# A two-layer graph network on one core: GpSimd's low-half subtraction in the build waits for VectorE's one-hots

## The chip, the core and the metric

The kernel runs on one core of a Trainium2 chip. The metric is the device time of one execution in microseconds (us). The core has five engines: TensorE (PE in the profile), VectorE (DVE), ScalarE (ACT), GpSimd (POOL) and SyncE (SP), which here issues the DMAs. Each runs its own list of instructions in order, and they wait for each other on semaphores.

## The reference

A graph of 3125 nodes with 256 features and 50,000 edges goes through two layers:

```python
def _layer(x, rows, cols, vals, W, b):              # vals = 1 / degree of the row
    neigh = segment_sum(vals[:, None] * x[cols], rows)
    cat = concatenate([x, neigh], axis=1)
    return relu(cat @ W.T + b)

h = _layer(_layer(x, src, dst, vals, W0, b0), src, dst, vals, W1, b1)
x = layernorm(x + h)
h_sparse = keep_32_largest(x @ W_neigh)
neigh = segment_sum(h_sparse[src], dst) / maximum(degree(dst), 1)
x = layernorm(x + x @ W_self + neigh)
```

## The kernel before

The nodes are 25 tiles of 125 (`NT`, `P`). All sums over neighbours are matrix products with the dense matrix of edge counts, `ct`, 3125 x 3125 in float16, that the kernel makes itself in its first part, the build (about 20 to 171 us). The layers then multiply `ct` with the features, which are kept as two float16 parts, high and low, side by side in `xs` (512 columns a tile).

The build has one round per tile (`fills` for TensorE, the branch under `total > E - 1` for VectorE, `quick_copies` for ScalarE, `split_a0` for GpSimd). In the round of tile t:

- VectorE makes four sets of one-hots for tile t + 1 (`quick_hots`, L663, a comparison of `iota128` with `jobs`, both in SBUF): a large one (125x1792) and three smaller ones (125x1536). Between them it copies two groups of transposed counts out of PSUM into `ct` (`tr_copy`, L820). The order is large one-hots, copy, three sets of one-hots, copy. Every set increments `win_hot`. In rounds 4 and 5 it also computes two low parts of weights (`w_low`, L815).
- TensorE multiplies the one-hots of tile t into counts (`fill`, L1388), transposes the counts of the tile before (`transposes`, L1468), computes the rows' own product with the first weights in float32 (`own_product`, L1502) and transposes the next tile of x (L1483).
- ScalarE copies the counts from PSUM to `slab` (L1095), half of the transposes to `ct` (L1134), the own product to `own` (`own_copy`, L1152) and the transposed x to `x_t` (L1139).
- GpSimd splits the second half of `own`, the scaled x, into its two parts in `xs`: a cast makes the high part (L542), a subtraction the low part (L544). The cast waits for ScalarE's copy (`own_copied`), the subtraction for the cast (`a0_hi`). The subtraction increments `a0_split`.
- SyncE stores `own` and `slab` to DRAM.

The split has `own` with two halves, so ScalarE's copy of tile t waits for the subtraction of tile t - 2:

```python
act.wait_ge(a0_split, t + 1)     # the count starts at 2
```

After the build TensorE starts the first layer's aggregation when `a0_split` shows 23 tiles done, and finishes it when all 25 are.

If the inputs don't fit the quick way (`total < E`), another branch builds the matrix; with these inputs it isn't entered.

Of the kernel before, what the change touches and what calls it, by code (L numbers as in the profile page):

```python
# [30 lines left out]
NT = N // P  # L31
# [14 lines left out]
FILLS = len(SETS)  # L46
# [35 lines left out]
def gnn(nc, x, src, dst, w0, b0, w1, b1, wself, wneigh, out):  # L82
    ctx = ExitStack()
    with ctx:
        sem_names = set()

        def sem(name):
            assert name not in sem_names
            sem_names.add(name)
            return ctx.enter_context(nc.semaphore(name))  # L90
# [186 lines left out]
        win_hot, win_done, win_read = sem("win_hot"), sem("win_done"), sem("win_read")  # L277
# [202 lines left out]
        def _(pool):  # L480
# [52 lines left out]
            def split_a0(t):  # L533

                pool.wait_ge(own_copied, t + 2)
                if t == 0:
                    pool.wait_ge(scale_ready, 1)
                    nc.gpsimd.tensor_tensor(own[:, 0, :], own[:, 0, :], scales[0:P, 1:2].broadcast_to([P, 2 * F]), ALU.mult
                                            ).then_inc(own_scaled, 1)
                    pool.wait_ge(own_scaled, 1)  # L540
                a0 = own[:, t % 2, F:2 * F]
                nc.gpsimd.tensor_copy(xs[:, t, 0:F], a0).then_inc(a0_hi, 1)  # L542
                pool.wait_ge(a0_hi, t + 1)
                nc.gpsimd.tensor_tensor(xs[:, t, F:2 * F], a0, xs[:, t, 0:F], ALU.subtract).then_inc(a0_split, 1)  # L544

            pool.sem_inc(a0_split, 2)
            for t in range(NT):
                split_a0(t)
# [43 lines left out]
        def _(dve):  # L592
# [10 lines left out]
            def whole_part(out, given, size, step):  # L603
                step(v.tensor_scalar(out, given, 1.0 / size, 0.5 / size - 0.5, ALU.mult, ALU.add))
                step(v.tensor_scalar(out, out, ROUND, -ROUND, ALU.add, ALU.add))
# [109 lines left out]
            def general_table():  # L715

                count = [0]

                def step(ins):
                    count[0] += 1  # L720
                    ins.then_inc(slow_step, 1)
                    dve.wait_ge(slow_step, count[0])

                dve.wait_ge(win_hot, 2 * FILLS)
                dve.wait_ge(win_done, FILLS)
                by_chunk = [edges_f[:, j, 0:EQ * P].rearrange("p (g q) -> p g q", g=EQ) for j in range(2)]
                whole_part(hi_f[:, 1], by_chunk[1], W, step)
                whole_part(hi_f[:, 0], by_chunk[0], P, step)
                step(v.scalar_tensor_tensor(key[:, :, :], hi_f[:, 1], float(NT * W - W), by_chunk[1], ALU.mult, ALU.add))
                step(v.scalar_tensor_tensor(srcp[:, :, :], hi_f[:, 0], -float(P), by_chunk[0], ALU.mult, ALU.add))  # L730
                step(v.scalar_tensor_tensor(key[:, :, :], hi_f[:, 0], float(W), key[:, :, :], ALU.mult, ALU.add))
                v.engine_nop().then_inc(edge_keys, 2)
                step(v.tensor_reduce(wlim[:, 1, :], hi_f[:, 1], X, ALU.max))
                step(v.tensor_reduce(wlim[:, 0, :], hi_f[:, 1], X, ALU.min))
                for j in range(2):
                    for g in range(EQ):
                        last = v.tensor_scalar(wdiag[:, j, g, :], identf[0:EG, 0:EG], wlim[:, j, g:g + 1], None, ALU.mult)
                last.then_inc(diag_ready, 1)
                dve.wait_ge(keys_t, 1)
                step(v.memset(key_t[:, CH:CH + G], -1.0))  # L740
                step(v.memset(srcp_t[:, CH:CH + G], 0.0))
                for out, b in ((srcp_t, bank[0]), (key_t, bank[1])):
                    step(v.tensor_copy(out[:, 0:CH].rearrange("p (e g) -> p g e", g=EQ),
                                       b[0:P, 0:CH].rearrange("p (g e) -> p g e", g=EQ)))

                dve.wait_ge(lims_b, 1)
                step(v.tensor_scalar(cover[:, :], bank[2][0:P, 0:CH], wcol[:, :], None, ALU.is_le))
                step(v.scalar_tensor_tensor(cover2[:, :], bank[3][0:P, 0:CH], wcol[:, :], cover[:, :], ALU.is_ge, ALU.mult))
                step(v.tensor_tensor(cover3[:, :], cover2[:, :], rev_f[:, :], ALU.mult))
                step(v.tensor_tensor(cover4[:, :], cover2[:, :], inc_f[:, :], ALU.mult))  # L750
                step(v.tensor_reduce(lim[:, 0:1], cover3[:, :], X, ALU.max))
                step(v.tensor_reduce(lim[:, 1:2], cover4[:, :], X, ALU.max))
                step(v.tensor_scalar(lim[:, 2:3], lim[:, 0:1], -1.0, float(CH), ALU.mult, ALU.add))
                step(v.tensor_tensor(lim[:, 3:4], lim[:, 1:2], lim[:, 2:3], ALU.subtract))
                step(v.tensor_scalar(lim[:, 4:5], lim[:, 3:4], 1.0 / G, (G - 1.0) / G + 0.5 / G - 0.5, ALU.mult, ALU.add))
                step(v.tensor_scalar(lim[:, 5:6], lim[:, 4:5], ROUND, -ROUND, ALU.add, ALU.add))
                v.tensor_scalar(lim[:, 6:7], lim[:, 5:6], 1.0, None, ALU.max).then_inc(win_lims, 1)

                dve.wait_ge(rows_t, 1)
                step(v.memset(rows[:, :, :], 0.0))  # L760
                step(v.memset(rows[:, 3, :], 1.0))
                step(v.tensor_copy(rows[:, 0, 0:NW], bank[4][0:1, 0:NW]))
                step(v.tensor_copy(rows[:, 2, 0:NW], bank[4][0:1, 128:128 + NW]))
                step(v.tensor_tensor_scan(rows[:, 1, 1:NW + 1], rows[:, 3, 0:NW], rows[:, 2, 0:NW], 0.0, ALU.mult, ALU.add))
                v.tensor_copy(table[:, :, :], rows[:, 0:2, :]).then_inc(table_ready, 1)
# [129 lines left out]
            with dve.If(total < E):  # L895
                general_table()
                clear_tr()
                bound_rows()
                bounds()
                scales_out()  # L900
                for u in range(WT):
                    general_hots(u)
                for i in range(4):
                    w_low(i)
                with dve.Fori(1, NT) as t:
                    for u in range(WT):
                        general_hots(t * WT + u)
                        if u == 1:
                            v.tensor_copy(xstage[:, :], xs32[:, ds(t - 1, 1), :].rearrange("p o f -> p (o f)")).then_inc(own_staged, 1)
                first_trees()  # L910
# [69 lines left out]
            for T in range(NT):  # L980
                b, K = T % 2, T - 3
                t = t2[(NT + T) % 2]
# [740 lines left out]
```

## Time and profile before

| | us |
|---|---|
| median of three runs | 665.47 |
| lowest, highest | 664.07, 667.5 |
| the profiled execution's own time | 663.18 |
| its span, first to last instruction | 661.4 |

| engine | busy us | share of the span |
|---|---|---|
| TensorE, matmuls | 629.1 | 95% |
| VectorE | 496.6 | 75% |
| ScalarE | 314.2 | 48% |
| GpSimd | 111.6 | 17% |

The shares are averages over parts with different limits. In the page's 40 slices VectorE and ScalarE are at nine tenths or more from the fifth slice to the tenth, within the build, and TensorE is so in nearly all slices. In a row in order of time the first number is the start in us from the span's start and the second how long the instruction, or the merged group of them, took. Records of instructions that follow each other closely on one engine overlap by some hundredths of a microsecond. What an engine waited for stands in brackets.

### The profile page before, as it was taken

The page shows a single profiled execution, that of the slowest core. Times are in us where ns is not written, and L with a number is a line of the kernel's source. Part 1 is how long each engine was busy: PE and PEld are TensorE (multiplying, and loading weights), DVE is VectorE, ACT ScalarE, POOL GpSimd, SP SyncE. Part 2 cuts the span into 40 slices and gives each one's busy share as a digit, 9 for nine tenths or more (in the row PEclk, how much of TensorE's full clock was granted, in tenths as well). Part 3 has the DMA queues.
Part 4 walks back from the last instruction along what each step waited for, and adds up shares of the span by engine and source line. Part 5 has one row for each costly group of instructions (what it writes and reads, how often), then busy time and mean ns, then how long its engine had stood idle before and what let it go on. Part 6 is the DMA issues. An engine that isn't in the chain of part 4 may idle for free.

```text
span 661.4 us, 10805 instructions
## 1 busy us (share of the span) xinstructions
PE 629.1 (95%) x3758; PEld 321.4 (49%) x3759; DVE 496.6 (75%) x1273; ACT 314.2 (48%) x606; POOL 111.6 (17%) x188
## 2 busy tenths in 40 slices
PE   7789999999888999999999999998999999999996
PEld 3466677666433444444444444444444444444442
DVE  7988999999688888888853687886888837533333
ACT  3779999999486676757641222222222200000000
POOL 3014222112211010101101223223232200000000
PEclk9989999999999999999999999999999999999999
DMA  9435655555422232322213999999999633300000
GB/s 230 90 116 154 223 182 173 169 179 181 134 50 64 51 67 49 67 51 64 55 45 110 204 180 186 196 175 204 181 196 189 152 97 115 111 25 27 24 24 24
DMA packets 66742, 79.62 MB, mean 120 GB/s; under 512 B 30320, under 2 KB 59407, under 8 KB 66681
## 3 DMA queue, kind: packets, MB, share of 16 engines
q1 hardware_dynamic: 66681, 78.86, 53.6%
q8 instruction: 32, 0.52, 0.4%
q14 instruction: 29, 0.24, 0.1%
HBM read 38.91 MB, written 33.38 MB: 109 GB/s over the span
## 4 chain that ended last, share of the span: by engine, by line
PE 54%; DVE 32%; DMA 6%; ACT 3%; issue 2%; POOL 2%; SPq 0%; ACTq 0%; DVEq 0%; POOLq 0%
PE pair L1575 22%; DVE hots L663 12%; PE bank L1673 11%; PE pair L1673 10%; DMA tr_sb<-part 5%; DVE ct L820 4%; PE pair L1476 3%; PE bank L1476 3%; DVE m L966 3%; DVE work L971 2%; PE bank L1502 1%; DVE tree L849 1%; DMA own_in<-own_dram 1%; POOL part L571 1%; PE bank L1468 1%
## 5 line engine op out<-in xcount | busy, mean ns | idle before, releaser
L1575 PE MATMUL pair<-xs,ct 125*128 125x512 f16 x625 | 139.5, 379 | 1.2 <-issue 1.2
L1575 PE MATMUL pair<-a,ct 125*128 125x512 f16 x625 | 138.9, 379 | 0.0
L663 DVE TENSOR_TENSOR hots<-iota,jobs 125x1792 f16<-125x1792 f16 (+1 forms) x100 | 103.1, 1066 | 0.8 <-ACT jobs L1077 0.7
L1575 PEld LDWEIGHTS pair<-a,ct 125*128 125x128 f16 x625 | 62.0, 99 | 73.8
L1575 PEld LDWEIGHTS pair<-xs,ct 125*128 125x128 f16 x625 | 61.7, 100 | 73.9 <-issue 1.7
L1254 ACT ACTIVATE a<-ct 125x1000 f16<-125x1000 f16 (+1 forms) x75 | 80.4, 1071 | 9.6 <-DMA c_dram<-slab 7.9
L1095 ACT ACTIVATE slab<-pair 125x875 f16<-125x875 f32 (+1 forms) x100 | 83.3, 860 | 3.1 <-PE pair L1388 1.6
L553 POOL TENSOR_TENSOR own_in<-own_in,bias_sb 125x256 f32<-125x256 f32 x50 | 38.5, 771 | 235.9 <-DMA own_in<-own_dram 235.8
L1673 PE MATMUL bank<-xs,ct 125*128 125x512 f16 (+1 forms) x325 | 71.5, 379 | 0.0
L1673 PE MATMUL pair<-xs,ct 125*128 125x512 f16 x300 | 66.2, 379 | 0.0
L1322 ACT ACTIVATE sd<-mv,epsb 125x1 f32<-125x1 f32 x25 | 7.4, 294 | 113.9 <-DVE mv L1028 113.9
L1468 PEld LDWEIGHTS bank<-ident,slab 125*128 125x128 f16 x625 | 39.6, 99 | 35.9 <-issue 22.1
L925 DVE SCALAR_TENSOR_TENSOR t<-pair,rdeg,own_in 125x256 f32<-125x256 f32 x50 | 24.1, 483 | 43.4 <-PE pair L1575 38.2
L1388 PE MATMUL pair<-hots 125*128 125x125 f16 x625 | 52.5, 223 | 3.9 <-DVE hots L663 3.1
L1468 PE MATMUL bank<-ident,slab 125*128 125x125 f16 x625 | 51.5, 220 | 4.8 <-ACT slab L1095 1.7
L1502 PE MATMUL bank<-w_t,x_t 128*125 128x512 f32 x100 | 53.6, 621 | 1.5 <-DVE sv L782 0.9
L1673 PEld LDWEIGHTS bank<-xs,ct 125*128 125x128 f16 (+1 forms) x325 | 32.3, 100 | 37.8
L1673 PEld LDWEIGHTS pair<-xs,ct 125*128 125x128 f16 x300 | 29.8, 99 | 34.9
L1388 PEld LDWEIGHTS pair<-hots 125*128 125x128 f16 x625 | 40.6, 100 | 7.7 <-issue 4.7
L1476 PE MATMUL bank<-w_lay,tr_sb 128*128 128x512 f16 x150 | 36.5, 379 | 4.6 <-DMA tr_sb<-part 4.5
L1476 PE MATMUL pair<-w_lay,tr_sb 128*128 128x512 f16 x150 | 36.5, 379 | 3.2 <-DMA tr_sb<-part 3.1
L820 DVE COPY ct<-bank 125x1008 f16<-125x1008 f16 x50 | 33.6, 671 | 7.6 <-PE bank L1468 7.6
(203 smaller groups left out, 750.2 us busy)
## 6 DMA issues: line engine op xcount, KB each, us to landing
c_dram<-slab SPq DMA_DIRECT2D x25, 683.6 KB
ct<-c_dram SPq DMA_DIRECT2D x25, 683.6 KB
own_in<-own_dram SPq DMA_DIRECT2D x50, 125.0 KB
own_dram<-own SPq DMA_DIRECT2D x25, 125.0 KB
own_dram<-own_st SPq DMA_DIRECT2D x25, 125.0 KB
x_in<-in_x_dram SPq DMA_DIRECT2D x25, 125.0 KB
z_dram<-z_st SPq DMA_DIRECT2D x25, 125.0 KB
a<-z_dram SPq DMA_DIRECT2D x5, 625.0 KB
```

Source lines behind the costliest of these rows:

```text
L553: nc.gpsimd.tensor_tensor(own_in[k % 2][:, :], own_in[k % 2][:, :], bias_sb[:, :], ALU.add).then_inc(own_biased, 1)
L663: v.tensor_tensor(hots[k][:, :, :, :].rearrange("p w g (a d) -> p (w g) a d", d=2), iota, job, ALU.is_equal).then_inc(win_hot, 1)
L820: v.tensor_copy(ct[:, TG0[g]:TG0[g] + TG[g], t, :], tr16[1][0:P, 0:TG[g], 0:PC]).then_inc(tr_free[1], 1)
L925: return noted(v.scalar_tensor_tensor(t2[k % 2][:, :], agg[k % 3][0:P, 0:F], rdeg[l][:, T:T + 1], own_in[k % 2][:, :], ALU.mult, ALU.add))
L1095: a.activation(slab3[t % 2][:, :, lo * QW:hi * QW].rearrange("p b (w d) -> p b w d", d=QW), pair[f % 2][0:P, 0:n, 0:QKEY].rearrange("p w ( ...
L1254: a.activation(unread[:, 0:(hi - lo) * P].rearrange("p (b s) -> p b s", s=P), ct[:, lo:hi, T, 0:P], ACT.Copy, accum_out=deg_part[:, T, k:k ...
L1388: last = mm(pair[f % 2][:, u, 0:QKEY], hots[f][:, u, 0, :], hots[f][:, u, 1, 1:QKEY + 1], start=True, stop=True, skip_group_check=True)
L1468: last = nc.tensor.transpose(tr16[g % 2][:, i, 0:P], slab[par][:, (TG0[g] + i) * P:(TG0[g] + i) * P + 128], ident16[:, 0:P])
L1476: last = mm(out, lhs(2 * pt + h), w[:, h, q, :], start=h == 0 and k == 0, stop=h == 1 and k == 2, skip_group_check=True)
L1502: last = mm(bank[6][0:P, :].rearrange("p (a f) -> p a f", a=2), x_t32[:, h, :], w0_t[:, h::2, :], start=h == 0, stop=h == 1, skip_group_ch ...
L1575: ins = mm(agg[k % 3][0:lhs.shape[1], :], lhs, parts[l][:, t, :], start=t == 0, stop=t == NT - 1, skip_group_check=True)
L1673: ins = mm(out3[T % 8][0:lhs.shape[1], :], lhs, xs[:, b, :], start=b == 0, stop=b == NT - 1, skip_group_check=True)
```

## The change

GpSimd's subtraction for tiles 4 to 23 waits, beside the cast before it, until `win_hot` has reached 4 (t + 2), that is, until VectorE has finished the fourth set of one-hots for tile t + 1. The branch that isn't entered raises the semaphore by itself, so that GpSimd doesn't wait there for ever. The order of the instructions on every engine stays.

```diff
@@ split_a0(t), GpSimd
                 nc.gpsimd.tensor_copy(xs[:, t, 0:F], a0).then_inc(a0_hi, 1)
                 pool.wait_ge(a0_hi, t + 1)
+                if 3 < t < NT - 1:
+                    pool.wait_ge(win_hot, FILLS * (t + 2))
                 nc.gpsimd.tensor_tensor(xs[:, t, F:2 * F], a0, xs[:, t, 0:F], ALU.subtract).then_inc(a0_split, 1)
@@ general_table(), VectorE
                 dve.wait_ge(win_hot, 2 * FILLS)
+                dve.sem_inc(win_hot, FILLS * NT)
                 dve.wait_ge(win_done, FILLS)
```

## Rows read from the trace of the kernel before

**Rows 1.** Busy time by window, 72.6 to 160.6 us: stretch, length, busy time by engine

```profile
72.60:160.60 88.00, 85.81 (x942) 60.59 (x940) 88.00 (x102) 84.36 (x135) 18.87 (x35) 1.00 0.58 181
```

**Rows 2.** Chain of waits over a tile: start, length, what

```profile
99.04 2.97 DVE hots L663 x3
102.01 0.59 DVE ct L820
102.61 1.00 DVE hots L663
```

**Rows 3.** Order of time, VectorE and GpSimd, the tile at 66 us

```profile
66.64 1.31 DVE L663 TENSOR_TENSOR hots<-iota,jobs 125x1536 f16<-125x1536 f16 x1
...
68.53 1.81 DVE L663 TENSOR_TENSOR hots<-iota,jobs 125x1536 f16<-125x1536 f16 x2
...
66.46 0.67 POOL L544 TENSOR_TENSOR xs<-own,xs 125x256 f16<-125x256 f32 x1
```

**Rows 4.** Order of time, VectorE and GpSimd, two steady tiles

```profile
98.37 0.67 DVE L820 COPY ct<-bank 125x1008 f16<-125x1008 f16 x1
98.96 3.05 DVE L663 TENSOR_TENSOR hots<-iota,jobs 125x1536 f16<-125x1536 f16 x3
...
104.12 3.08 DVE L663 TENSOR_TENSOR hots<-iota,jobs 125x1536 f16<-125x1536 f16 x3
...
98.31 0.40 POOL L542 CAST xs<-own 125x256 f16<-125x256 f32 x1 [4.00 <-ACT own L1152]
98.79 0.67 POOL L544 TENSOR_TENSOR xs<-own,xs 125x256 f16<-125x256 f32 x1
...
103.98 0.67 POOL L544 TENSOR_TENSOR xs<-own,xs 125x256 f16<-125x256 f32 x1
```

**Rows 5.** Order of time, VectorE and GpSimd, the tiles at 60 and 156 us

```profile
60.97 1.16 DVE L815 SCALAR_TENSOR_TENSOR w_parts<-w_t,scales,w_parts 128x512 f16<-128x512 f32 x1
...
64.38 0.74 DVE L815 SCALAR_TENSOR_TENSOR w_parts<-w_t,scales,w_parts 128x512 f16<-128x512 f32 x1
...
155.86 3.24 DVE L663 TENSOR_TENSOR hots<-iota,jobs 125x1536 f16<-125x1536 f16 x3
...
60.30 1.29 POOL L544 TENSOR_TENSOR xs<-own,xs 125x256 f16<-125x256 f32 x1
...
156.16 1.26 POOL L544 TENSOR_TENSOR xs<-own,xs 125x256 f16<-125x256 f32 x1
```

**Rows 6.** All instructions of line L820: shortest, median, longest in ns

```profile
L820 DVE COPY ct<-bank x50: 662/670/684, 37.2 to 170.5; 125x1008 f16<-125x1008 f16 x50
```

**Rows 7.** Order of time, VectorE, the large one-hots of rounds 6 and 23

```profile
71.52 1.08 DVE L663 TENSOR_TENSOR hots<-iota,jobs 125x1792 f16<-125x1792 f16 x1
...
159.62 1.07 DVE L663 TENSOR_TENSOR hots<-iota,jobs 125x1792 f16<-125x1792 f16 x1
```

**Rows 8.** Order of time, where GpSimd answers VectorE

```profile
46.05 0.15 DVE L801 COPY scales<-bank 128x16 f32<-128x16 f32 x1
...
46.36 1.04 POOL L538 TENSOR_TENSOR own<-own,scales 125x512 f32<-125x512 f32 x1 [27.33 <-DVE scales L801]
...
170.46 0.68 DVE L820 COPY ct<-bank 125x1008 f16<-125x1008 f16 x1 [0.78 <-PE bank L1468]
...
171.26 1.10 POOL L559 MEMSET part<- 32x512 f16 x2 [4.36 <-DVE ct L820]
```

**Rows 9.** Order of time, ScalarE and TensorE in one tile

```profile
102.72 0.72 ACT L1152 ACTIVATE own<-bank,scales 125x512 f32<-125x512 f32 x1
103.61 0.38 ACT L1139 ACTIVATE x_t<-bank 128x250 f32<-128x250 f32 x1 [0.17 <-PE bank L1483]
...
102.75 0.60 PE L1468 MATMUL bank<-ident,slab 125*128 125x125 f16 x8
```

**Rows 10.** Chain of waits at the end of the build

```profile
159.84 0.60 PE bank L1468 x8
...
165.00 0.60 PE bank L1468 x8
```

## The prediction

> **What bounds the kernel now.** I first looked at the page's busy shares in slices, to see which engines are full in the build, the part that the change touches. Then I read the busy times by window over that part [rows 1]: in 88.0 us VectorE is busy for all 88.00, ScalarE for 84.36, and TensorE for 85.81, which is a modelled number. The chain of waits over one tile says the same in another way [rows 2]: the only owners are VectorE's three one-hot instructions (2.97 us together), the copy out of PSUM (0.59), the one large one-hot (1.00), and the second copy. So in the build a microsecond that VectorE loses is a microsecond of the kernel, as long as no other engine becomes the bound.
>
> Next I put VectorE's and GpSimd's instructions in order of time beside each other. In the tile at 66 us [rows 3] GpSimd's subtraction runs from 66.46 to 67.13 in its usual 0.67. The one-hots that start at 66.64 inside it take 1.31 us, while the next two, with GpSimd silent, take 1.81 for both. Records overlap by about 0.07, so one clean instruction takes 0.94 and three clean ones take 1.81 + 0.87 = 2.68. VectorE lost 1.31 - 0.94 = 0.37. The steady tiles show the same [rows 4]: three one-hots take 3.05 beside a subtraction that began 0.17 before them, and 3.08 beside one that began 0.14 before them. That is a loss of 0.37 to 0.40, and in other tiles 0.36 to 0.41; I take 0.385. The loss is what was left of the subtraction when the one-hots began, less about 0.06. Two other tiles show the reverse order [rows 5]. There the subtraction starts inside a one-hot instruction, is itself stretched (1.29 and 1.26 for 0.67), gets in when that instruction ends, and delays VectorE's following one: by 1.16 - 0.74 = 0.42 in the tile at 60 us and by 3.24 - 2.68 = 0.56 in the tile at 156 us.
>
> The copy out of PSUM doesn't mind. All 50 lie between 662 and 684 ns [rows 6], though GpSimd's 0.40 us cast and the first part of its subtraction run beside one of them in every tile, themselves at their usual time [rows 4].
>
> **The change, part by part.** It adds one wait, on the count of one-hots, to 20 subtractions (tiles 4 to 23). The subtraction of tile t now starts when the fourth set of one-hots of tile t + 1 is done. In VectorE's order the copy of the other transposes follows there, then the large one-hot of the next tile, so the subtraction leaves the three one-hots and lies beside a copy.
>
> What it removes: in tiles 4 and 5, 0.42 and 0.37. For tiles 6 to 22 I take the distance from one large one-hot to the same one 17 tiles later [rows 7]: 159.62 - 71.52 = 88.10 us, or 5.18 a tile. Sixteen of these lose 0.385 and one loses 0.56: 6.72 us. In tile 23 VectorE's one-hots are no longer on the chain of waits, so nothing is counted there.
>
> What it adds: the subtraction starts some time after the fourth one-hots. GpSimd has answered VectorE twice near the build [rows 8]: a small copy ended at 46.20 and GpSimd started at 46.36, and a copy ended at 171.14 and GpSimd started at 171.26. So the start is 0.12 to 0.16 after, and the end 0.79 to 0.83 after. The copy's share of the chain is 0.59, and then the large one-hot wants to start. By the 0.06 found above its delay is 0.14 to 0.18; I take 0.15. No row shows a subtraction in this place, so the bounds are 0 (the copy covers it whole) and 0.25 (an answer 0.1 slower).
>
> VectorE's time for the 17 tiles becomes 88.10 - 6.72 + 17 x 0.15 = 83.93, or 4.94 a tile.
>
> What is late next: ScalarE idles (88.00 - 84.36) / 17 = 0.21 a tile [rows 1], so from there it needs 4.97; its records overlap by about 0.1 where nothing is waited for, so the true need is a little less, near 4.92. Its one wait is before its copy of the transposed x [rows 9]: TensorE's eight transposes start 0.15 after VectorE's copy (102.60 to 102.75), the transposes of x come behind them, and ScalarE starts at 103.61, 0.17 after it had finished. That wait moves forward with VectorE, so it shrinks. VectorE's 4.94 and ScalarE's 4.92 are almost equal, and I take 4.95 for the tile: 17 x 4.95 = 84.15, a gain of 3.95. Tiles 4 and 5 give 0.42 + 0.37 - 2 x 0.15 = 0.49. There VectorE also splits weights and has no idle time, so it all counts. The last tile runs by TensorE and ScalarE from one group of eight transposes to the next, 165.00 - 159.84 = 5.16 [rows 10]; at 4.95 it gives 0.2. Together 3.95 + 0.49 + 0.2 = 4.6 us.
>
> Behind the waiting subtraction GpSimd has the cast of the next tile, which comes about 3 us after the new start of the subtraction. ScalarE's copy of tile t + 2 waits for the subtraction of tile t; it is given up a whole tile ahead of its need, since `own` has two halves. The wait itself costs GpSimd nothing that matters, because it idles most of each tile. The 25th tile keeps its old order, so the layer's start isn't held up. The added increment in the general branch isn't executed. Everything after the build hangs on its end through the chain of waits, so I pass the gain through whole.
>
> The profiled execution took 663.18 us (span 661.38 and 1.8 around it), so its successor would take 658.6. It lies 2.3 under the median of the three runs, 665.47; against that median the forecast is 660.9. With the added delay at 0 the one-hots' loop is faster than ScalarE, the tile takes 4.92, and the gain is 4.46 + 0.79 + 0.24 = 5.5. With 0.25 a tile takes 5.04, and the gain is 2.5 + 0.3 + 0.1 = 2.9.
>
> **The rivals.**
>
> *The other engines keep the pace.* If the fixed answers between VectorE, TensorE and ScalarE leave half of ScalarE's wait in place, a tile takes about 5.10: 17 x 0.08 + 0.49 + 0.05 = 1.9 gained, 663.6. For it speaks that three loops lie within 0.05 us of each other; against it, that the wait before ScalarE follows VectorE's copy directly.
>
> *The cast takes the place.* The cast (0.40) sits in the shelter of the copy today [rows 4]. If ScalarE's copy of the own product comes 0.5 later against VectorE's order, the cast falls on the first one-hots and costs 0.40 - 0.06 = 0.34. A tile would take 4.94 + 0.34 = 5.28, 0.1 more than now: +1.7 for the 17 tiles less 0.2, so 667.0. Against it: the drift would have to be larger than ScalarE's whole idle time.
>
> *The subtraction comes in front of the large one-hot.* This is the slower side. If the subtraction runs only once the copy has ended, the large one-hot waits for all of it: 0.67 - 0.06 = 0.61 a tile. 17 x 0.61 - 6.72 = +3.65, and in tiles 4 and 5 2 x 0.61 - 0.79 = +0.43: 669.6. It decides from the point where the subtraction starts over 0.38 us after the fourth one-hots (0.38 + 0.67 - 0.06 - 0.59 = 0.40, today's loss); the two answers in the trace are 0.12 and 0.16. The other way to it would be a copy that holds GpSimd off; the rows beside it say no [rows 4, 6]. The Trainium skill (SBUF — State Buffer, Who interferes with whom) lists `copy` among the operations that can take the port pair shared with GpSimd, and says that the loser of it blocks fully. Taken alone that would give this rival's 669.6; the same page ties it to operand conditions, and this copy reads PSUM. The trace stands against it: cast and subtraction keep 0.40 and 0.67 beside the copy.
>
> *There is nothing to remove.* If the stretched one-hots had another cause than the subtraction, their loss would stay and the time would be 665.5. [...] The trace disagrees: 0.94 alone and 1.31 beside a subtraction, and 1.29 for a subtraction of 0.67 [rows 3, 5].
>
> **How the numbers follow.** A measurement of this kernel can tell about 0.5%, 3.3 us, from no change. The forecast has 0.73, the pace of the other engines 0.11, the cast 0.05, the subtraction in front of the large one-hot 0.06, nothing to remove 0.05. Of the forecast's 0.73 I put 0.06 within 0.5%, since its low end gains 2.9. Faster: 0.67. Within 0.5%: 0.06 + 0.11 + 0.05 + 0.05 = 0.27. Slower: 0.06. The range starts at the largest gain, 5.5 under the median, less the 1.4 by which the fastest of the three runs lies under it, rounded in by 0.3: 658.3. It ends at 665.2, where the forecast's low end (662.6) with the 2.0 of the slowest run over the median, and the rival of the other engines' pace (663.6) with most of it, are inside.
>
> **What the profile would show.** Right: three one-hots at 2.68 in tiles 6 to 22, subtractions of 0.67 beginning about 0.15 after the fourth one-hots, beside a copy of 0.67, the large one-hot at about 1.2 for 1.07, a tile of 4.95, and ScalarE's wait before the copy of the transposed x nearly gone. Wrong: a subtraction stretched to over 1 us or a large one-hot near 1.7 (the slower side); one-hots at 3.05 with no subtraction beside them (nothing to remove); one-hots stretched beside the cast; VectorE idle before its copies with tiles over 5.05 (another engine's pace); or a gain in the build that is lost between its end and that of the kernel.

## The result, and the profile after

| | before | after |
|---|---|---|
| median, us | 665.18 (10 runs) | 661.09 (10 runs) |
| lowest, highest | 663.06, 669.77 | 659.55, 662.98 |
| the profiled execution's span | 661.4 | 658.1 |

The ratio of the times is 0.9938, with a 95% interval of 0.9916 to 0.9961: 4.1 us faster. The forecast was 4.6 us faster, at 660.9. The medians here and below leave out four slow executions, one each of e3_write_only, e5_short_own, e6_gate_from_3 and the kernel before, run beside the last two.

First VectorE and GpSimd in order of time, in two steady tiles of the changed kernel. They answer to [rows 4].

```profile
97.48 2.68 DVE L665 TENSOR_TENSOR hots<-iota,jobs 125x1536 f16<-125x1536 f16 x3
100.08 0.67 DVE L823 COPY ct<-bank 125x1008 f16<-125x1008 f16 x1
100.67 1.25 DVE L665 TENSOR_TENSOR hots<-iota,jobs 125x1792 f16<-125x1792 f16 x1
101.85 0.67 DVE L823 COPY ct<-bank 125x1008 f16<-125x1008 f16 x1
102.44 2.68 DVE L665 TENSOR_TENSOR hots<-iota,jobs 125x1536 f16<-125x1536 f16 x3
...
100.31 0.67 POOL L546 TENSOR_TENSOR xs<-own,xs 125x256 f16<-125x256 f32 x1 [2.73 <-DVE hots L665]
102.12 0.40 POOL L542 CAST xs<-own 125x256 f16<-125x256 f32 x1 [1.14 <-ACT own L1155]
```

Three one-hots take 2.68, as when nothing is beside them. The subtraction begins at 100.31, 0.15 after the fourth one-hots ended at 100.16. It runs beside the copy and reaches 0.3 into the large one-hot, which takes 1.25 for 1.07.

The window that answers to [rows 1] (stretch, length, then busy time of TensorE, its weight loads, VectorE, ScalarE and GpSimd):

```profile
72.60:155.60 83.00, 82.53 (x928) 60.62 (x929) 82.94 (x101) 82.32 (x134) 18.29 (x33) 1.00 0.60 188
```

ScalarE idles 0.68 in 83 us, where it idled 3.64 in 88. All three engines are full now. In the chain of waits over a tile, the counterpart of [rows 2], VectorE is gone and TensorE holds every piece, one right behind the other (start, length, what):

```profile
100.37 0.91 PE bank L1505 x2
101.28 0.44 PE bank L1471 x8
```

That doesn't make TensorE the bound. Where three engines are all full, the chain stays on the one on which it is entered; over 98 to 109 us of e1_third the same view names ScalarE alone. The pace is told by the starts. TensorE in order of time:

```profile
98.74 1.08 PE L1505 MATMUL bank<-w_t,x_t 128*125 128x512 f32 x2
...
103.67 1.07 PE L1505 MATMUL bank<-w_t,x_t 128*125 128x512 f32 x2
```

TensorE's round takes 4.93 here, while VectorE's large one-hots (100.67 and, not shown, 105.63) stand 4.96 apart. TensorE is making up a delay that is told below; from about 136 us on its rounds take 4.95 to 4.96 too. So it is still VectorE that sets the steady tile: 4.79 with nothing stretched, and 0.17 for the large one-hot.

The large one-hots of rounds 6 and 23, in order of time, answer to [rows 7]:

```profile
70.75 1.08 DVE L665 TENSOR_TENSOR hots<-iota,jobs 125x1792 f16<-125x1792 f16 x1
...
155.22 1.25 DVE L665 TENSOR_TENSOR hots<-iota,jobs 125x1792 f16<-125x1792 f16 x1
```

They stand 84.47 us apart, where they stood 88.10 apart: 3.63 us in 17 tiles. The first took 4.78, since its large one-hot (70.75) isn't stretched, and two were disturbed. The first of the two in order of time:

```profile
84.72 0.92 ACT L1098 ACTIVATE slab<-pair 125x875 f16<-125x875 f32 x1 [0.68 <-DMA c_dram<-slab]
...
87.21 2.88 DVE L665 TENSOR_TENSOR hots<-iota,jobs 125x1536 f16<-125x1536 f16 x3
...
87.44 0.97 POOL L542 CAST xs<-own 125x256 f16<-125x256 f32 x1 [1.69 <-ACT own L1155]
```

ScalarE waited 0.68 for the store of an earlier slab, so its copy of the own product came late, and the cast behind it fell on the one-hots: 2.88 for 2.68. That is the rival of the cast, once in 20 tiles. This tile took 5.16. The next took 5.11, because TensorE was late and VectorE's copy behind the large one-hot waited for its transposes (0.14). Together the two lost 0.35.

### The profile page after: what moved, and what is told of

Its sections match the earlier page's. It is cut to its first block, busy times and chain, and to the rows that moved or that the text cites. A ratio compares the mean times of both kernels' runs of the same rounds, so it can differ in the third digit from the quotient of the medians.

```text
span 658.1 us, 10825 instructions
## 1 busy us (share of the span) xinstructions
PE 627.2 (95%) x3758; PEld 322.1 (49%) x3759; DVE 492.5 (75%) x1273; ACT 313.2 (48%) x606; POOL 111.5 (17%) x188
## 4 chain that ended last, share of the span: by engine, by line
PE 64%; DVE 16%; DMA 8%; ACT 6%; issue 3%; POOL 2%; SPq 1%; ACTq 0%; DVEq 0%; POOLq 0%
PE pair L1578 22%; PE bank L1676 11%; PE pair L1676 10%; PE bank L1505 5%; DMA tr_sb<-part 5%; PE bank L1471 4%; PE pair L1391 4%; PE bank L1479 3%; PE pair L1479 3%; DVE m L969 3%; DVE work L974 2%; ACT slab L1098 2%; DMA own_in<-own_dram 1%; POOL part L573 1%; DVE tree L852 1%
## 5 line engine op out<-in xcount | busy, mean ns | idle before, releaser
L665 DVE TENSOR_TENSOR hots<-iota,jobs 125x1792 f16<-125x1792 f16 (+1 forms) x100 | 99.1, 1027 | 0.7 <-ACT jobs L1080 0.7
L852 DVE TENSOR_TENSOR tree<-tree,ct 125x630 uint16<-125x630 uint16 x75 | 38.4, 511 | 2.6
```

Source lines behind the costliest of these rows:

```text
L665: v.tensor_tensor(hots[k][:, :, :, :].rearrange("p w g (a d) -> p (w g) a d", d=2), iota, job, ALU.is_equal).then_inc(win_hot, 1)
L852: step(v.tensor_tensor(tree[:, :], tree[:, :], quint[k], ALU.add))
```

## The experiments

Eleven kernels ran. In the profile of each I read one number that hardly depends on what happens elsewhere: the distance over 17 tiles, from the large one-hot of round 6 to that of round 23. The ratios and intervals are those on record; they are not the quotients of the medians beside them.

| kernel | 17 tiles, us | a steady tile | median, us | ratio to before, interval |
|---|---|---|---|---|
| before | 88.10 | 5.16 to 5.19 | 665.2 | |
| the change | 84.47 | 4.96 | 661.09 | 0.9938 [0.9916, 0.9961] |
| e7_change_again | 84.11 | 4.96 | 661.46 | 0.9956 [0.9933, 0.9979] |
| e1_third | 83.84 | 4.92 | 661.12 | 0.9946 [0.9920, 0.9972] |
| e6_gate_from_3 | 83.54 | 4.93 | 661.79 | 0.9950 [0.9927, 0.9973] |
| e3_write_only | 83.73 | 4.93 | 659.79 (4 runs) | 0.9934 [0.9903, 0.9964] |
| e5_short_own | 83.74 | 4.93 | 659.83 (3 runs) | 0.9906 [0.9874, 0.9939] |
| e10_short_product | 82.06 | 4.82 | 659.44 | 0.9916 [0.9884, 0.9947] |
| e11_both_short | 82.57 | 4.79, up to 132 us | 656.85 (4 runs) | 0.9892 [0.9845, 0.9938] |
| e2_second | 88.56 | 5.26 | 665.96 | 1.0027 [1.0002, 1.0052] |
| e4_late | 88.05 | 5.20 | 664.55 | 0.9992 [0.9971, 1.0014] |
| e8_later | 86.53 | 4.99 and 5.29 in turn | 663.45 | 0.9983 [0.9964, 1.0002] |
| e9_cast_gated | 87.52 | 5.16 | 664.60 | 0.9993 [0.9972, 1.0014] |

The median of the kernel before, run beside them, was 665.22, 665.21 and 664.94 in the three groups. In e3_write_only, e5_short_own, e10_short_product and e11_both_short a part of the work is left out, so their times are no measure of the change.

### Is the conflict one of reads?

```diff
-                nc.gpsimd.tensor_tensor(xs[:, t, F:2 * F], a0, xs[:, t, 0:F], ALU.subtract).then_inc(a0_split, 1)
+                if 3 < t < NT - 1:
+                    nc.gpsimd.memset(idle[:, :], 0.0)
+                    nc.gpsimd.memset(xs[:, t, F:2 * F], 0.0).then_inc(a0_split, 1)
```

This edit is made to the kernel before (its other tiles keep the subtraction), without the gate.

> The kernel before, without the gate; in tiles 4 to 23 two memsets (320 and 256 float16 a partition) stand in the place of the subtraction, so the low half is zero there. GpSimd is busy as long as with the subtraction, over the start of the first of the three one-hots, but only writes. Theory (the conflict is over reads: one-hots have two inputs in SBUF, the subtraction too): no one-hots are stretched, three take 2.68 and the large one 1.07; the tile is ScalarE's and TensorE's 4.93, the kernel 4.5 to 5.5 us faster than before. Rival (any GpSimd work on SBUF stretches VectorE): three one-hots at 3.0 and the time of the kernel before.

VectorE and GpSimd in order of time, in e3_write_only:

```profile
106.67 2.69 DVE L668 TENSOR_TENSOR hots<-iota,jobs 125x1536 f16<-125x1536 f16 x3
...
106.42 0.40 POOL L543 CAST xs<-own 125x256 f16<-125x256 f32 x1 [3.86 <-ACT own L1157]
106.87 0.36 POOL L546 MEMSET idle<- 125x320 f16 x1
107.17 0.31 POOL L547 MEMSET xs<- 125x256 f16 x1
```

GpSimd writes from 106.87 to 107.48, inside the first of the one-hots, where a subtraction is held and then delays the next. Neither is stretched: the memsets take 0.36 and 0.31, the one-hots 2.69, as alone. So GpSimd's being busy doesn't stretch VectorE; the subtraction, which reads two inputs from SBUF, does. The Trainium skill (SBUF — State Buffer, Who interferes with whom) states that a VectorE instruction with two SBUF inputs contends with a GpSimd instruction that reads SBUF, and not with one that only writes. The trace agrees: 2.69 for three one-hots beside memsets here, and 1.31 for 0.94 for one beside a subtraction in [rows 3]. A memset differs from a subtraction in more than its reads, so this run alone doesn't prove that it is them; e9_cast_gated below adds that a cast, which reads one input, is held as well. The kernel was 5.4 us faster than before by the medians and 4.4 by the ratio; expected were 4.5 to 5.5.

### What the place costs: the gate earlier and later

The gate one set earlier (e1_third; in e2_second the last line has - 2, two sets earlier):

```diff
-                    pool.wait_ge(win_hot, FILLS * (t + 2))
+                    pool.wait_ge(win_hot, FILLS * (t + 2) - 1)
```

> The gate opens one set earlier, at the third of the four sets of one-hots. Theory (the one who comes second waits for the running instruction, then goes first): the subtraction arrives about 0.15 us after the fourth set has begun, is held to about 1.5 us in its record, gets in as the fourth set ends and runs beside the copy, about 0.1 us earlier than with the gate at the fourth. The three smaller one-hots stay at 2.68, the large one falls from 1.25 to 1.10 or less. VectorE then needs about 4.8 a tile, ScalarE and TensorE 4.93, so the tile takes 4.93 to 4.95 for 4.97 and the kernel 0.3 to 0.7 us less than the change. Rival (VectorE alone bounds the tile): 4.80 a tile, 2.9 us less than the change. Rival (a held subtraction stretches VectorE's instruction): three one-hots at 3.05, time as before the change.

In order of time, in e1_third:

```profile
104.06 0.68 DVE L823 COPY ct<-bank 125x1008 f16<-125x1008 f16 x1
104.66 2.69 DVE L665 TENSOR_TENSOR hots<-iota,jobs 125x1536 f16<-125x1536 f16 x3
107.28 0.67 DVE L823 COPY ct<-bank 125x1008 f16<-125x1008 f16 x1
107.87 1.07 DVE L665 TENSOR_TENSOR hots<-iota,jobs 125x1792 f16<-125x1792 f16 x1
109.00 0.68 DVE L823 COPY ct<-bank 125x1008 f16<-125x1008 f16 x1
...
106.63 1.25 POOL L546 TENSOR_TENSOR xs<-own,xs 125x256 f16<-125x256 f32 x1 [1.83 <-DVE hots L665]
```

The subtraction arrives at 106.63 inside the fourth one-hots, is held, and ends at 107.88, just as the large one-hot begins at 107.87. Nothing of VectorE's is stretched: 2.69 and 1.07. The distance from the large one-hot to the copy behind it is now 1.13, not 1.00, because the copy waits for TensorE, whose eight transposes begin at 108.35 and take 0.60. The tile is 4.92 and not VectorE's 4.80, so the first rival falls. In whole times it can't be told from the change (661.12 and 661.09).

> The gate opens two sets earlier, at the second of the four sets. Theory: the subtraction arrives while the third set runs, is held, and runs just before the fourth, which loses 0.56 as at 156 us in the kernel before. Three one-hots take about 3.24, the large one 1.07, a tile 5.35: 0.17 x 17 = 2.9 us more than the kernel before for tiles 6 to 22, about 668. Rival (only the share of time that the two overlap counts, whatever the order): the loss is at most today's 0.385 and the time that of the kernel before.

In order of time, in e2_second:

```profile
103.49 3.15 DVE L665 TENSOR_TENSOR hots<-iota,jobs 125x1536 f16<-125x1536 f16 x3
...
104.58 1.25 POOL L546 TENSOR_TENSOR xs<-own,xs 125x256 f16<-125x256 f32 x1 [1.35 <-DVE hots L665]
```

The order of events is as expected, but the loss is 3.15 - 2.68 = 0.47, not 0.56. The held subtraction ended at 105.83, so it ran from 105.16, 0.14 before the record of the instruction that held it ends; in the one tile at 156 us, from which the 0.56 came, it was 0.05 before. A price read from a single disturbed tile was 0.09 too high. The tile of 5.26 is still above the kernel before, against the rival, and the kernel is slower by 0.3%: the only one of the eleven whose interval lies above 1, if barely. Expected was about 668; it took 665.96, because the loss was smaller and the first tiles took 4.79.

The gate where it is, and the subtraction held back behind it by memsets that only write (the first in e4_late and e8_later, the second in e8_later alone):

```diff
                     pool.wait_ge(win_hot, FILLS * (t + 2))
+                    nc.gpsimd.memset(idle[:, 0:256], 0.0)
+                    nc.gpsimd.memset(idle[:, 256:320], 0.0)
```

> The changed kernel with a memset of 256 float16 a partition (about 0.3 us, into a tile that nothing reads) between the gate and the subtraction, which so starts about 0.5 us after the fourth one-hots. Theory: the large one-hot waits for nearly the whole subtraction and takes 1.07 + 0.5 = 1.6; three one-hots 2.68; a tile 5.30; for tiles 6 to 22 that is 2 us more than the kernel before and 5.6 more than the change: about 667.5. Rival (the wait's place doesn't matter as long as the one-hots are spared): 4.97 a tile, as with the change.

In order of time, in e4_late:

```profile
105.50 1.49 DVE L667 TENSOR_TENSOR hots<-iota,jobs 125x1792 f16<-125x1792 f16 x1
...
105.10 0.31 POOL L547 MEMSET idle<- 125x256 f16 x1 [3.06 <-DVE hots L667]
105.37 0.67 POOL L548 TENSOR_TENSOR xs<-own,xs 125x256 f16<-125x256 f32 x1
```

The fourth one-hots ended at 104.98, so the subtraction begins 0.39 after, not 0.5, and the prediction's formula gives 0.39 + 0.67 - 0.06 - 0.59 = 0.41. Measured: 1.49 - 1.07 = 0.42. The formula held; my expected start was wrong by 0.1. A tile is 5.20, not 5.30, and the kernel is equal to the kernel before, not 2 us slower. So a quarter of a microsecond in GpSimd's answer is worth the whole gain.

> As e4_late, where the subtraction began 0.39 us after the fourth one-hots and the large one-hot took 1.49; a second memset of 64 float16 delays it by another 0.1 or so, to 0.50. Theory (loss = start + 0.67 - 0.06 - 0.59): the large one-hot takes 1.07 + 0.52 = 1.59, a tile 5.31, and the kernel 2 us more than the kernel before. If the start comes after 0.59 instead, the large one-hot has begun, holds the subtraction off and takes 1.07; the subtraction runs beside the copy that follows, and the tile takes 4.92 to 4.96. Rival (0.42 was the most that the place can cost): 1.49 and 5.21 as in e4_late.

In order of time, in e8_later:

```profile
99.52 1.58 DVE L668 TENSOR_TENSOR hots<-iota,jobs 125x1792 f16<-125x1792 f16 x1
...
104.81 1.07 DVE L668 TENSOR_TENSOR hots<-iota,jobs 125x1792 f16<-125x1792 f16 x1
...
106.40 2.01 DVE L668 TENSOR_TENSOR hots<-iota,jobs 125x1536 f16<-125x1536 f16 x2
...
104.77 1.65 POOL L549 TENSOR_TENSOR xs<-own,xs 125x256 f16<-125x256 f32 x1
106.36 1.24 POOL L543 CAST xs<-own 125x256 f16<-125x256 f32 x1
```

Here both expected cases occur in one run. In the tile at 99 us the large one-hot takes 1.58, and the next begins at 104.81: 5.29, as expected. In that next tile the subtraction is recorded from 104.77, almost at the same moment as the large one-hot, loses, is held to 106.42 and costs the large one-hot nothing (1.07). But the cast behind it is late now and costs the following one-hots 0.20 (2.01 for 1.81). Such tiles come in turn, 5.29 and then 4.99. The mean tile is 5.09, and the kernel is 1.8 us under before, within noise of it (the interval ends at 1.0002), and not 2 over. The slower side that I had put at 669.6 was not reached: just short of its full price the two engines arrive together and VectorE may go first. What decides it, the records don't tell: in the tile at 99 us, too, the subtraction's record (99.48, not shown) begins 0.04 before that of the large one-hot, and there it went first.

### The cast in the wrong place

```diff
+                if 3 < t < NT - 1:
+                    pool.wait_ge(win_hot, FILLS * (t + 2) - 2)
                 nc.gpsimd.tensor_copy(xs[:, t, 0:F], a0).then_inc(a0_hi, 1)
```

> The changed kernel with GpSimd's cast gated as well, at the second set of one-hots, so that it arrives while the third is running; the subtraction keeps its gate at the fourth. Theory (a cast is no cheaper in the wrong place than a subtraction is: it is held, then goes before the next one-hots for 0.40 less 0.1 to 0.2): the cast's record is stretched to about 1.0, the fourth one-hots lose 0.2 to 0.3, the large one stays at 1.25, a tile takes 5.16 to 5.26, 3.4 to 5 us more than the change over tiles 6 to 22: near the kernel before. Rival (a cast has one input and is too short to matter): 4.96 a tile.

In order of time, in e9_cast_gated:

```profile
101.96 2.88 DVE L667 TENSOR_TENSOR hots<-iota,jobs 125x1536 f16<-125x1536 f16 x3
...
103.03 0.99 POOL L544 CAST xs<-own 125x256 f16<-125x256 f32 x1 [2.54 <-DVE hots L667]
```

The cast is held (0.99 for 0.40) and takes 2.88 - 2.68 = 0.20 from VectorE, at the low end of what was expected. A tile is 5.16, and the gain of the change is gone (ratio 0.9993). The subtraction's move pays only as long as the cast keeps its shelter. The prediction had priced this rival at 0.34 a tile, by the subtraction's 0.06; held, the cast costs 0.20. Nor does the 0.06 fit a cast that isn't held: in e3_write_only the cast ran until 106.82, 0.15 into the one-hots from 106.67, and they took 2.69, no more than a hundredth over.

### What holds the tile at 4.92

The gate stays at the third set in the next three, so that VectorE has nothing stretched. In e5_short_own ScalarE copies half as much of the own product; in e10_short_product the second of TensorE's float32 products for it has 32 columns; e11_both_short has both.

```diff
-                a.activation(own[:, par, :], bank[6][0:P, :], ACT.Copy, scale=scales[0:P, 1:2]).then_inc(own_copied, 1)
+                lo = F if isinstance(t, int) and 3 < t < NT - 1 else 0
+                a.activation(own[:, par, lo:], bank[6][0:P, lo:], ACT.Copy, scale=scales[0:P, 1:2]).then_inc(own_copied, 1)
```

> The gate at the third set, as in e1_third, where a tile takes 4.92 us and VectorE waits about 0.1 in it; here ScalarE's copy of the own product leaves out its first half (256 of 512 columns) in tiles 4 to 23, so that these rows' own part is an older tile's. It is there 0.2 to 0.3 us shorter, and TensorE's and VectorE's work is as before. Theory (ScalarE is the next bound, TensorE's own round needs 4.81, VectorE's 4.79): a tile takes 4.80 to 4.84, about 1.7 us less than e1_third in tiles 6 to 22. Rival (TensorE's round with its fixed answers holds the tile): 4.90 to 4.92, and the same time as e1_third.

ScalarE and VectorE in order of time, in e5_short_own:

```profile
102.95 0.38 ACT L1142 ACTIVATE x_t<-bank 128x250 f32<-128x250 f32 x1 [0.16 <-PE bank L1487]
...
101.60 1.08 DVE L665 TENSOR_TENSOR hots<-iota,jobs 125x1792 f16<-125x1792 f16 x1
...
106.53 1.08 DVE L665 TENSOR_TENSOR hots<-iota,jobs 125x1792 f16<-125x1792 f16 x1
```

ScalarE's instruction is 0.2 shorter, and all of it turns into a wait for TensorE (0.16). The tile stays at 4.93. The theory, that ScalarE was next, falls, and the rival stands.

```diff
-                last = mm(bank[6][0:P, :].rearrange("p (a f) -> p a f", a=2), x_t32[:, h, :], w0_t[:, h::2, :], start=h == 0, stop=h == 1,
-                          skip_group_check=True)
+                n = 16 if h == 1 and isinstance(t, int) and 3 < t < NT - 1 else F
+                last = mm(bank[6][0:P, :].rearrange("p (a f) -> p a f", a=2)[:, :, 0:n], x_t32[:, h, :], w0_t[:, h::2, 0:n],
+                          start=h == 0, stop=h == 1, skip_group_check=True)
```

> The gate at the third set, and in tiles 4 to 23 the second of TensorE's two float32 products for the own part has 32 columns for 512, so that the rest of those columns lacks half its sum; TensorE's round is about 0.8 us shorter. ScalarE's and VectorE's work is whole. Theory (ScalarE's round is 4.92 by itself too, as close as TensorE's): a tile still takes 4.90 to 4.92. Rival (TensorE alone held the tile in e5_short_own): 4.80 a tile, which VectorE then sets.

VectorE in order of time, and the window, in e10_short_product:

```profile
102.39 1.08 DVE L665 TENSOR_TENSOR hots<-iota,jobs 125x1792 f16<-125x1792 f16 x1
...
107.21 1.08 DVE L665 TENSOR_TENSOR hots<-iota,jobs 125x1792 f16<-125x1792 f16 x1
```
```profile
75.50:150.00 74.50, 68.18 (x866) 55.67 (x865) 74.50 (x93) 73.86 (x123) 25.34 (x31) 1.00 0.61 194
```

The tile falls to 4.82 with ScalarE's work whole, and VectorE is busy for all of the 74.50 us. So ScalarE needs no more than 4.82. With e5_short_own, where less work for ScalarE changed nothing, it was TensorE that held the tile at 4.92.

> Both shortenings at once: ScalarE's copy of the own product without its first half, as in e5_short_own, and TensorE's second product with 32 columns for 512, as in e10_short_product, with the gate at the third set. Theory: each of the two holds a tile at 4.92, so only both together free it, and VectorE's 4.79 to 4.80 decides (all its instructions back to back); about 2 us less than e1_third over tiles 6 to 22. Rival (a fixed answer between engines is in the loop): above 4.85 with idle time on all three.

TensorE in order of time, in e11_both_short:

```profile
103.88 0.60 PE L1472 MATMUL bank<-ident,slab 125*128 125x125 f16 x8 [0.42 <-DVE ct L823]
```

TensorE waits 0.42 for VectorE's copy in this tile, and a tile is 4.79, which is the sum of VectorE's instructions with nothing stretched. The value that the theory gave is right, but not its reason, since e10 had already freed the tile to within 0.03. In e10 the 17 tiles come to 82.06, just over 17 times the steady tile (81.9). In e11 they come to 82.57 against 81.4, because the pace was lost. At 127 us ScalarE waited 1.07 for a store, the cast came late, and in the next four rounds it lay on the one-hots:

```profile
134.33 2.88 DVE L665 TENSOR_TENSOR hots<-iota,jobs 125x1536 f16<-125x1536 f16 x3
...
139.32 2.88 DVE L665 TENSOR_TENSOR hots<-iota,jobs 125x1536 f16<-125x1536 f16 x3
```

The last four tiles took 5.40, 4.98, 5.00 and 4.99. With so little idle time on any engine, a single late store moved the cast out of its shelter, and it got back only at 154 us.

### The rest

```diff
-                if 3 < t < NT - 1:
-                    pool.wait_ge(win_hot, FILLS * (t + 2))
+                if 2 < t < NT - 1:
+                    pool.wait_ge(win_hot, FILLS * (t + 2) - 1)
```

> The gate at the third set and also for tile 3, whose subtraction now stretches a large one-hot of that round (1.59 for 1.08). Theory: in that round VectorE waits over 1 us for TensorE's transposes shortly after, so the 0.5 us goes into that wait: time of e1_third within 0.3 us, and tiles of 4.92. Rival (VectorE is on the path there too): 0.5 us less than e1_third.

VectorE and GpSimd in order of time, in e6_gate_from_3:

```profile
56.49 1.60 DVE L665 TENSOR_TENSOR hots<-iota,jobs 125x1792 f16<-125x1792 f16 x1
...
56.47 0.67 POOL L546 TENSOR_TENSOR xs<-own,xs 125x256 f16<-125x256 f32 x1
```

The edit did not do what it was made for. The cast of tile 3 came late (55.99), so the gate was already open when the subtraction got to it, and the large one-hot took 1.60, for 1.59 in the kernel before. Neither the theory nor the rival is tested; the run is one more of e1_third. It agrees with it: tiles of 4.93, a median of 661.79 for 661.12, and intervals that overlap almost wholly.

> The changed kernel once more, as it is, to have it on the chip of these runs. Theory: 4.96 a tile in tiles 6 to 22, the large one-hot at 1.25, three one-hots at 2.68, ratio to the kernel before 0.993 to 0.995. Rival (the measured 4.1 us was partly scatter of the part behind the build): a ratio nearer 1, with the build as short as before.

The change again gave 0.9956, its interval reaching from 0.9933 to 0.9979, with a steady tile of 4.96. That is 2.9 us by the ratio and 3.8 by the medians, for 4.1 in the first measurement. The ratio lies just outside the 0.993 to 0.995 that I expected, on the rival's side. The build is as short in both (84.11 and 84.47), and the two intervals have 0.9933 to 0.9961 in common, 2.6 to 4.5 us. So some of the 4.1 may have been scatter behind the build; the runs don't decide it.

## Why the prediction was right

Its mechanism and its main sizes held, by its own steps:

- **What the subtraction cost.** Taken as 0.385 a tile. With the one-hots spared they take 2.68, as the prediction had worked out from the clean rows, and with e3_write_only's memsets in its place they take 2.69. Right.
- **What it costs in the new place.** Taken as 0.15, between 0 and 0.25. The large one-hot takes 1.25 or so for 1.07, 0.17 to 0.18, with the start at 0.15. e4_late confirmed the formula behind it at another start (0.41 for 0.42).
- **The tile.** Taken as 4.95; the steady tile is 4.96, and VectorE sets it. The 17 tiles gained 3.63 for a forecast of 3.95. The missing 0.32 are 0.17 for the hundredth in each tile and 0.35 for the two disturbed tiles, less 0.18 for the first tile, within rounding.
- **Tiles 4 and 5, and the last.** From the copy at 59.51 to the large one-hot at 71.52 before, 12.01; from 59.29 to 70.75 after, 11.46: 0.55 gained for 0.49. From the last large one-hot to the start of the last copy, 10.84 before (170.46 - 159.62) and 10.66 after (165.88 - 155.22): 0.18 for 0.2. The build's gain is 3.63 + 0.55 + 0.18 = 4.4 for 4.6.
- **Passed through whole.** The two profiled executions differ by 3.3, not 4.4: from the last copy to the end they took 490.9 before and 492.2 after. In the eleven experiments' profiles the same stretch lies between 490.8 (e1_third) and 493.0 (e6_gate_from_3), whatever the gate, so 1.3 is scatter. The medians, 4.1 apart, agree with whole passage, but an interval of 2.6 to 5.6 us would allow a good part of the 4.4 to be lost.
- **What is late next.** Here the reason was wrong, and the number stood by luck. The prediction put ScalarE's need at about 4.92 and called it the next bound. e5_short_own and e10_short_product show that ScalarE needs no more than 4.82, and that it is TensorE, with its instructions back to back, that needs 4.92. I had looked at ScalarE's idle time and taken TensorE's busy time as too roughly modelled to count. Its instructions' starts, which aren't modelled, would have told in the kernel before. TensorE in order of time:

```profile
100.14 1.08 PE L1502 MATMUL bank<-w_t,x_t 128*125 128x512 f32 x2
101.05 0.39 PE L1468 MATMUL bank<-ident,slab 125*128 125x125 f16 x4
...
101.60 1.07 PE L1502 MATMUL bank<-w_t,x_t 128*125 128x512 f32 x2
```

The transposes follow the first product 0.91 after its start. Behind the second product, as long as the first, they start at 102.75 [rows 9], 1.15 after it: a wait of 0.24 in a tile of 5.16, so a need of 4.92. That it equals the 4.92 put down for ScalarE is chance. In the change itself neither was met, since VectorE's 4.96 is longer; the forecast's largest gain, with the tile at 4.92, rested on it.
- **The slower rival.** Its decision point, a start 0.38 after the fourth one-hots, was right: at 0.39 (e4_late) the gain is gone. Its full price of 0.61 a tile was not reached in any run; e8_later shows why. The copy did not hold GpSimd off: the subtraction began 0.15 after the one-hots and kept its 0.67 beside the copy. So the reading by which such a copy holds GpSimd off fails here, as the prediction had argued.
- **The range.** 665.47 less 5.5 and 1.4 is 658.6. The 658.3 lies 0.3 further out, where the prediction says rounded in; nothing hangs on it.

## What to carry to other kernels

Where VectorE is full, look in the order of time at what GpSimd reads beside each VectorE instruction with two SBUF inputs: the loss there was what was left of GpSimd's instruction, less a little, and a copy out of PSUM beside it lost nothing. A semaphore wait can move the small instruction into such a shelter, and the place decides: the gate at the second set costs 0.47 a tile, ungated 0.385, at the fourth 0.17, at the third nothing. Before counting the gain, find the second-slowest engine by its instructions' starts, not by its idle time alone; with the gate at the third set it took 0.13 of the 0.385. And look at what else has to stay in its shelter when everything is full: one late store cost the kernel two longer tiles, and e11_both_short four.

## What was not expected of the hardware

The time in which a GpSimd instruction is held is not lost if what follows is sheltered. In e1_third the held subtraction ends 0.53 after the record of the fourth one-hots. If it runs for its usual 0.67 once it gets in, it gets in 0.14 before that record ends, while a subtraction that waits for their semaphore starts 0.15 after it and ends 0.82 after it. Being held was 0.29 us quicker than being told.

The granted clock differed from execution to execution of nearly the same program, and with it the start of the build. The page's row of the granted clock (tenths in 40 slices), of e9_cast_gated and then of e1_third:

```profile
PEclk9879999999999999999999999999999999999999
```
```profile
PEclk9879999999999999999999899999999999999999
```

In both the second and third slices are lower than before the change, where the row began 9989. The large one-hot of round 3, ahead of every gated subtraction, starts at 53.15 and 52.70, for 49.94 before and 49.72 after. In the six profiles with 9989 it starts between 49.7 and 50.0, in the seven others between 51.4 and 53.2. So 1.5 to 3.4 us of the scatter between single executions, nearly as large as the effect under study, arises before the gated tiles. e1_third shows a further slow stretch between 360 and 380 us, where the windows give a granted clock of 0.91, for 1.00 in the changed kernel. What sets it off, these runs don't show.
